# A routing stage rewritten: all x loads ahead, no mask, and GpSimd in VectorE's place for half of the normalisation

## What is computed

```python
xn = _layernorm(x)                       # (x - mean) / sqrt(var + 1e-5)
logits = xn @ gate_w.T + gate_b          # 4096 x 8
scores = softmax(logits)
top_w, top_i = top_k(scores, 2)
gate_dense = sum(one_hot(top_i, 8) * top_w[..., None], axis=1)
def expert(w1e, b1e, w3e, b3e, w2e, b2e):
    h = silu(xn @ w1e.T + b1e) * (xn @ w3e.T + b3e)
    return h @ w2e.T + b2e
y = einsum('etd,te->td', outs_of_8_experts, gate_dense)
out = x + time_mix(xn) + y + shared_expert(xn)
```

## Time and profile before

| what | us |
|---|---|
| median of 3 runs | 500.8 |
| lowest, highest | 498.76, 504.41 |
| span of the profiled execution, first to last instruction | 476.0 |
| median less that span (what lies around it) | 24.8 |
| `route` ends (`tile_tok` written) | 69.1 |

### The profile page before, as it was taken

One profiled execution on the slowest core, in us unless ns is written; L12 is line 12 of the kernel. 1 busy time (PEld: TensorE's weight loads), 2 busy tenths in 40 slices (PEclk: granted clock), 3 DMA queues, 4 the chain that ended last, 5 costly groups with the idle time before them and its releaser, 6 DMA issues.

```text
span 476.0 us, 8336 instructions
## 1 busy us (share of the span) xinstructions
PE 442.4 (93%) x2532; PEld 370.7 (78%) x2532; DVE 370.7 (78%) x700; ACT 241.5 (51%) x396; POOL 235.9 (50%) x222
## 2 busy tenths in 40 slices
PE   0886987988999999999999899999999999999997
PEld 0652464877888888888888778898898989898987
DVE  6967896968788898788776589996868687877863
ACT  4684845488586685958565633332414132423131
...
GB/s 182 281 349 330 277 88 91 105 140 180 270 232 160 216 209 185 115 152 101 145 189 122 250 323 90 228 104 152 125 148 123 121 150 132 154 108 72 23 23 44
DMA packets 45858, 77.24 MB, mean 162 GB/s; under 512 B 5908, under 2 KB 32252, under 8 KB 45820
## 3 DMA queue, kind: packets, MB, share of 16 engines
...
## 4 chain that ended last, share of the span: by engine, by line
PE 46%; POOL 17%; DVE 14%; issue 13%; ACT 4%; DMA 4%; SPq 0%; POOLq 0%; DVEq 0%; ACTq 0%
POOL xg L1008 8%; PE ps_w L1545 5%; PE ps_w L1547 5%; PE ps_w L1546 5%; PE ps_w L1611 5%; PE ps_w L1610 5%; PE ps_w L1612 5%; PE ps_g L1085 4%; DMA w_lo<-w_all 2%; POOL den L1020 2%; PE ps_y L1085 2%; POOL den L1019 2%; DVE stats L678 2%; POOL col L1027 2%; POOL firsts L1027 2%
## 5 line engine op out<-in xcount | busy, mean ns | idle before, releaser
L1008 POOL DMA_INDIRECT xg<-xn_rows,tile_tok x71 | 72.7, 1024 | 20.7 <-issue 18.5
L1521 POOL DMA_INDIRECT yg<-expert_rows,rows x64 | 67.8, 1060 | 23.6 <-issue 17.1
L1085 PE MATMUL ps_g<-w_hi,x_hi 128*128 x142 | 56.2, 396 | 1.9 <-DVE x_lo L1240 1.9
L1085 PE MATMUL ps_g<-w_lo,x_hi 128*128 x142 | 56.3, 396 | 0.0
L1085 PE MATMUL ps_g<-w_hi,x_lo 128*128 x142 | 56.1, 395 | 0.0
L1652 ACT ACTIVATE sact<-ps_w,vec_b 128x512 f32<-128x512 f32 x32 | 22.0, 687 | 58.2 <-PE ps_w L1547 58.2
L1545 PE MATMUL ps_w<-col_hi,s_hi 128*128 128x512 f32 x128 | 50.5, 395 | 0.4 <-DVE shid L1763 0.4
L1546 PE MATMUL ps_w<-col_lo,s_hi 128*128 128x512 f32 x128 | 50.2, 392 | 0.0
L1547 PE MATMUL ps_w<-col_hi,s_lo 128*128 128x512 f32 x128 | 50.2, 392 | 0.0
L1085 PE MATMUL ps_y<-w_hi,h_hi 128*128 x142 | 43.1, 304 | 1.3 <-DVE h_lo L1256 1.3
L1249 DVE TENSOR_TENSOR hid<-ps_g,act 128x512 f32<-128x512 f32 (+1 forms) x36 | 23.7, 657 | 24.6 <-ACT act L1161 24.6
...
## 6 DMA issues: line engine op xcount, KB each, us to landing
...
```

The costliest lines, as they stand in the source:

```text
L1008: pool.indirect_dma_start(out=xg[b][:, t, :], out_offset=None, in_=xn_d[:, :], in_offset=bass.IndirectOffsetOnAxis(ap=tile_tok[:, first_ti ...
L1085: mm = nc.tensor.matmul(out, x[:, k, :], w[:, ds(e, 1), k, cols].rearrange("p o n -> p (o n)"), start=(k == 0 and n == 0), stop=(last and ...
L1521: pool.indirect_dma_start(out=yg[a.buf(2)][:, k, q, :], out_offset=None, in_=y_d[:, :], in_offset=bass.IndirectOffsetOnAxis(ap=picked[a.bu ...
```

## The change

It rewrites `route` alone.

- x has 8 buffers' worth of room (`NX = NSTEP`): the four `xin`, and the two `y` buffers, `firsts1` and `terms`, lent until the experts need them. Steps 0 to 3 are loaded first, then the small inputs, then 4 to 7; only step 7 waits, for `xin[0]`.
- GpSimd scales the two groups that VectorE scaled (L508 in the changed kernel, `norm` of `gpsimd`). From step 3 on a `less_first` follows each. The zeroing of `terms` comes behind them all.
- The added 1e-5 is a bias of ScalarE's root, so VectorE's `var` operation goes. VectorE's constants come behind the statistics of step 0. Statistics have four buffers.
- There is no `mask`: TensorE sums both `hot` parts (bf16) in one accumulation, and ahead of all four `less`. The matrix `before` is 0 and -1, so that the total is subtracted in the same product. The slot is then one addition, one product of both choices and one sum.
- `share` is done once, after the one-hot rounds; ScalarE's exponents come behind its weight work, and `dense` behind `tile_tok`.
- Weight pieces are loaded up to two after each step (`SOON`).

```diff
-        NX, NN = 4, 4
+        NX, NN = NSTEP, 4
         MADE, BOTH, HIGH, LOW = 4, 6, 13, 2
         xT = [sb(f"xT{b}", [P, KC, STEP], F32) for b in range(NSTEP)]
-        xin = [sb(f"xin{b}", [P, Q, C], F32) for b in range(NX)]
+        xin = [sb(f"xin{b}", [P, Q, C], F32)[:] for b in range(4)]
+        lent = [[t[:] for t in y], [firsts1[:, b] for b in range(B)],
+                [terms[:].rearrange("p j n -> p (j n)")[:, b * HALF * C:(b + 1) * HALF * C]
+                 .rearrange("p (h c) -> p h c", h=HALF) for b in range(B)]]
+        LAST_X = NX - 1
+
+        def half(buf, b):
+            if 4 <= buf < LAST_X:
+                return lent[buf - 4][b]
+            return xin[buf % LAST_X][:, b * HALF:(b + 1) * HALF, :]
+
+        def group(buf, q):
+            return half(buf, q // HALF)[:, q % HALF, :]
+
         xn = [sb(f"xn{b}", [P, Q, C + 1], F32) for b in range(NN)]
 
-        SOON = 6
...
+        SOON = [0, 1, 2, 4, 6, 8, 10, 12, 14]
         ARRIVAL = [4, 5, 6, 7, 0, 1, 2, 3] + list(range(8, E * KC))
...
             def load_x(a):
 
-                at_least(sp, s_xn, a.i - NX + 1)
-                at_least(sp, s_xna, a.i - NX + 1)
+                if a.i == LAST_X:
+                    sp.wait_ge(s_xn, 1)
+                    sp.wait_ge(s_xna, 1)
                 for b in range(B):
-                    sp.dma_start(xin[a.buf(NX)][:, b * HALF:(b + 1) * HALF, :],
+                    sp.dma_start(half(a.buf(NX), b),
                                  xv[ds(a.i, 1), :, b, :, :].rearrange("o p h c -> p (o h) c")
                                  ).then_inc(s_xin[a.buf(NX)], 16)
 
...
-            load_x(At(0, 0, NSTEP))
-            load_x(At(0, 1, NSTEP))
+            for i in range(4):
+                load_x(At(0, i, NSTEP))
...
-            for i in range(2, NX):
+            for i in range(4, NSTEP):
                 load_x(At(0, i, NSTEP))
 
             def step(a):
...
-                if a.i + NX < NSTEP:
-                    load_x(a.plus(NX))
...
-                if a.i + SOON >= NSTEP:
-                    load_w(ARRIVAL[a.i + SOON - NSTEP])
+                for i in ARRIVAL[SOON[a.i]:SOON[a.i + 1]]:
+                    load_w(i)
...
-            nc.gpsimd.memset(terms[:], 0.0).then_inc(s_terms, 1)
-            pool.wait_ge(s_terms, 1)
-            nc.gpsimd.memset(terms[:, :, 3 * E:3 * E + 2], 1.0).then_inc(s_terms, 1)
-
             pool.wait_ge(s_negl, 32)
             nc.gpsimd.tensor_scalar(w_neg[:], w_neg[:], -1.0, None, ALU.mult).then_inc(s_neg, 1)
             pool.wait_ge(s_neg, 1)
             pool.dma_start(nw_d, w_neg[0:2 * E, :]).then_inc(s_negd, 16)
 
-            pool.wait_ge(s_negd, 16)
-            pool.wait_ge(s_lane, 4)
-            for i in range(MADE, E * KC):
+            def norm(a):
+                pool.wait_ge(s_scl, a.i + 1)
+                at_least(pool, s_T, a.i - NN + 1)
+                at_least(pool, s_xout[a.buf(NN)], a.uses(NN) * 32)
+                for q in range(DQ):
+                    ins = nc.gpsimd.tensor_scalar(xn[a.buf(NN)][:, q, 0:C], group(a.buf(NX), q),
+                                                  mv[a.buf(4)][:, q, 0:1], rstd[a.buf(4)][:, q:q + 1],
+                                                  ALU.subtract, ALU.mult)
+                ins.then_inc(s_xn, 1)
+
+            SINCE = 3
+            for i in range(NSTEP):
+                norm(At(0, i, NSTEP))
+                if i == SINCE:
+                    pool.wait_ge(s_negd, 16)
+                    pool.wait_ge(s_lane, 4)
+                if i >= SINCE:
+                    less_first(pool, MADE + i - SINCE)
+            for i in range(MADE + NSTEP - SINCE, E * KC):
                 less_first(pool, i)
+            pool.wait_ge(s_xn, LAST_X)
+            pool.wait_ge(s_xna, LAST_X)
+            nc.gpsimd.memset(terms[:], 0.0).then_inc(s_terms, 1)
+            pool.wait_ge(s_terms, 1)
+            nc.gpsimd.memset(terms[:, :, 3 * E:3 * E + 2], 1.0).then_inc(s_terms, 1)
...
-            nc.scalar.activation(early[:], gb[:], ACT.Exp)
-            exps(0, 0, EARLY)
             turned(At(0, NSTEP - 1, NSTEP))
             logit(len(GROUPS) - 1)
-            exps(1, EARLY, NSTEP)
-            act.wait_ge(s_second, 2)
-            nc.scalar.activation(gates[:, 1, :], behind[:], ACT.Exp).then_inc(s_gate, 1)
+            act.wait_ge(s_lane, 1)
+            nc.scalar.activation(lane_b[:], lane[:, :, None].broadcast_to([P, P, BATCH]), ACT.Copy
+                                 ).then_inc(s_lane, 1)
             for i in range(MADE):
                 made_hi(act, i)
             for i in range(4):
                 made_lo(act, i)
                 split(MADE + i)
-            nc.scalar.activation(early[:], gb[:], ACT.Silu)
+            nc.scalar.activation(early[:, 0:1], gb[:], ACT.Exp)
+            exps(0, 0, EARLY)
+            exps(1, EARLY, NSTEP)
+            act.wait_ge(s_second, 2)
+            nc.scalar.activation(gates[:, 1, :], behind[:], ACT.Exp).then_inc(s_gate, 1)
+            nc.scalar.activation(early[:, 1:2], gb[:], ACT.Silu)
+            act.wait_ge(s_xn, NSTEP)
+            act.wait_ge(s_xna, NSTEP)
...
+            pe.wait_ge(s_mask, 2)
+            for h, sums in enumerate((before, ones)):
+                for k in range(TOPK):
+                    mm = nc.tensor.matmul(ps_cnt[:, h, :].rearrange("p (e j) -> p e j", e=E), sums[:],
+                                          hot[:, k].rearrange("p j e -> p e j"), start=(k == 0), stop=(k == TOPK - 1))
+            mm.then_inc(s_cnt, 1)
             pe.wait_ge(s_firsts, 2)
             pe.wait_ge(s_Lg, len(GROUPS))
-            for i in range(2):
-                less(i)
-            pe.wait_ge(s_mask, 2)
-            nc.tensor.matmul(ps_cnt[:, 0, :], before[:], mask[:].rearrange("p e j -> p (e j)"),
-                             start=True, stop=True)
-            nc.tensor.matmul(ps_cnt[:, 1, :], ones[:], mask[:].rearrange("p e j -> p (e j)"),
-                             start=True, stop=True).then_inc(s_cnt, 1)
-            for i in range(2, MADE):
+            for i in range(MADE):
                 less(i)
             for i in range(4):
...
             def norm(a):
                 own = OwnIn(dve, s_dve, a, 1)
+                dve.wait_ge(s_var, a.i + 1)
                 dve.wait_ge(s_std, a.i + 1)
-                at_least(dve, s_xna, a.i - 1)
-                own.link(nc.vector.reciprocal(rstd[a.buf(2)][:], std[a.buf(2)][:]))
+                at_least(dve, s_xna, a.i - 3)
+                at_least(dve, s_xn, a.i - 3)
+                own.link(nc.vector.reciprocal(rstd[a.buf(4)][:], std[a.buf(4)][:]))
                 own.close()
-                nc.vector.scalar_tensor_tensor(out=less[a.buf(2)][:], in0=mv[a.buf(2)][:, :, 0], scalar=-1.0,
-                                               in1=rstd[a.buf(2)][:], op0=ALU.mult, op1=ALU.mult).then_inc(s_scl, 1)
-
-                at_least(dve, s_T, a.i - NN + 1)
-                at_least(dve, s_xout[a.buf(NN)], a.uses(NN) * 32)
-                for q in range(DQ):
-                    ins = nc.vector.tensor_scalar(xn[a.buf(NN)][:, q, 0:C], xin[a.buf(NX)][:, q, :],
-                                                  mv[a.buf(2)][:, q, 0:1], rstd[a.buf(2)][:, q:q + 1],
-                                                  ALU.subtract, ALU.mult)
-                ins.then_inc(s_xn, 1)
+                nc.vector.scalar_tensor_tensor(out=less[a.buf(4)][:], in0=mv[a.buf(4)][:, :, 0], scalar=-1.0,
+                                               in1=rstd[a.buf(4)][:], op0=ALU.mult, op1=ALU.mult).then_inc(s_scl, 1)
...
-                own.link(nc.vector.tensor_tensor(hot[1][:, t], work2[:, t], wide(red[:, t]), ALU.is_equal))
-                nc.vector.tensor_tensor(mask[:].rearrange("p e j -> p j e")[:, t], hot[0][:, t], hot[1][:, t],
-                                        ALU.add).then_inc(s_mask, 1)
-
-            def share(n, first_step, last_step):
-                t = slice(first_step * Q, last_step * Q)
-                count = (last_step - first_step) * Q
-                dve.wait_ge(s_exp, n + 1)
-                own.link(nc.vector.tensor_reduce(red[:, t], score[:, t], AX_X, ALU.add))
-                own.link(nc.vector.reciprocal(gates[:, 0, t], red[:, t]))
-                own.mark(nc.vector.tensor_tensor(score[:, t], score[:, t],
-                                                 gates[:, 0, t][:, :, None].broadcast_to([P, count, E]), ALU.mult))
+                nc.vector.tensor_tensor(hot[:, 1, t], work2[:, t], wide(red[:, t]), ALU.is_equal
+                                        ).then_inc(s_mask, 1)
+
+            def share():
+                dve.wait_ge(s_exp, 2)
+                own.link(nc.vector.tensor_reduce(red[:], score, AX_X, ALU.add))
+                own.link(nc.vector.reciprocal(gates[:, 0, :], red[:]))
+                own.mark(nc.vector.tensor_tensor(score, score, gates[:, 0, :, None].broadcast_to([P, NT, E]),
```

(23 more changed lines are left out.)

123 lines of the change are left out of this document (61 added, 62 removed).

## The result

| | us |
|---|---|
| the kernel before, in the runs beside it | 502.61 median (498.76 to 504.87, 4 runs) |
| the changed kernel | 511.57 median (510.26 to 512.44, 4 runs) |
| ratio, with its 95% interval | 1.0179 (1.0141 to 1.0218) |
| profiled execution of the changed kernel: time, span | 510.26, 508.4 |

A forecast was written before the change was run, and what follows sets the result against it. TensorE, busy 442.4 of 476.0 us, was taken as the bound, so only `tile_tok` mattered. No gain in the norm steps and `tile_tok` 0.8 us later gave a span of 476.8, plus 24.8, 501.6 us; range 497 to 506.

The forecast's parts named there:

- I take 0.82, since the factors come per partition as in that row: Norm steps: scaling one group on GpSimd costs 0.82 us, 1.64 a pair against VectorE's 0.73.
- GpSimd and TensorE both arriving at 35.0: End of the norm steps: both engines reach step 7 at about 35.0 us against 35.20 before, counted as no gain.
- The head: Start of the norm steps: `w_neg` issued 2.0 us later, GpSimd's first scaling at 12.6 us, TensorE beginning 2.1 us later.
- GpSimd becomes the pace: Slower rival, norm steps: GpSimd's chain has no slack; at 1.1 us a group the total is 506 us; chance 0.20.
- 1.9 us a pair: GpSimd's scaling by the Trainium skill's ratio: 2.1 us more than the sum if GpSimd paces, total 503.7 us; chance 0.07.
- Its landing took 1.35 us: Load of `w_neg`: from the last issue's end at 8.7 us, GpSimd starts to negate it at 10.0.
- twice the 0.65 us: Counts on TensorE: four matmuls instead of two take 1.25 us, from 44.8 to 46.0 us.
- TensorE in the way of the one-hot products: Between counts and one-hot products: eight weight pieces take 11.9 us, first product at 57.9 us against 56.94 before.
- TensorE warm, -1.3: Lower bound behind the counts: all four pieces at 1.48 us, first one-hot product at 56.6, 1.3 us off the total.
- The tail: From first one-hot product to `tile_tok`: VectorE's last operation ends at about 67.8, then 1.5 us, `tile_tok` at about 69.9.
- One to one into the end: Start of the experts: every microsecond `tile_tok` is ready sooner or later goes one to one into the end.
- 24.8 us above the profiled span: Whole kernel: the median of the runs is 24.8 us above the profiled span (500.8 - 476.0), kept constant.

The follow-up runs named there:

- less_late: The changed kernel with all of GpSimd's weight pieces behind its eight norm steps; ratio 1.0107 to the kernel before.
- after_fill4: The changed kernel with overwritten matrix products in TensorE's waits, one ahead of the last logits and four ahead of the counts; ratio 1.0131 to the kernel before.
- vec_fill4: The changed kernel with VectorE scaling again and overwritten products in TensorE's waits, one ahead of the last logits, four ahead of the counts; ratio 0.9958.
- no_idle1: vec_two with one overwritten matrix product in each of TensorE's two waits ahead of the counts; ratio 0.9886 to the kernel before.
- neg_early: The changed kernel with the loads of `w_neg` issued behind x steps 0 and 1, ahead of 2 and 3; ratio 1.0223 to the kernel before.
- gpsimd_only: The kernel before with only GpSimd's scaling, a weight piece after each of steps 3 to 7, and four buffers for the factors; ratio 1.0208.
- one_op: The changed kernel with one operation in GpSimd's scaling, the mean not subtracted; ratio 1.0179 to the kernel before.
- vec_scale: The changed kernel with the scaling of the two row groups given back to VectorE; ratio 1.0060 to the kernel before.
- before_again: The kernel before, unaltered, profiled a second time; span 495.0 us, time 496.7 us.
- vec_two: The changed kernel with VectorE scaling again and two of TensorE's four weight pieces ahead of the counts; ratio 0.9999 to the kernel before.

## Why the prediction was wrong, point by point

- **The step that failed: "I take 0.82, since the factors come per partition as in that row".** A group costs 1.21 us. The sum had GpSimd and TensorE both arriving at 35.0; measured, GpSimd alone sets the last turn, at 41.9. Of the 6.9 us between, the price of the scaling is 5.3: the first four pairs took 9.67 us where the sum had 7.1, and each of four cycles of pair and weight piece 4.25 where it had 3.57. The head below adds 2.2, and a weight piece that came sooner than assumed gives 0.5 back (its place of 20.5 us was itself a slip: 14.4 + 2.5 + 4 is 20.9). From there the lateness only travelled on: the counts were 6.6 us behind the forecast, the first one-hot product 7.3, `tile_tok` 7.3. The rival "GpSimd becomes the pace" named the mechanism, and its 1.1 us a group with 506 us was nearly the size; I gave it 0.20. By the forecast's own slope, 1.6 us for each 0.1, 1.21 would have made it 507.8.
- **Price and place.** Scaling at 2.42 us a pair was not the pace by itself: in less_late, with no weight pieces between, GpSimd waits for factors and TensorE sets the steps. It is pair plus weight piece in one queue, 4.25 us, and the late start. The cleanest price of who scales, in this order, is after_fill4 against vec_fill4, the same kernel but for that: 8.9 us at `tile_tok`, ratios 1.0131 and 0.9958.
- **The page.** The Trainium skill ("GPSIMD Engine Reference", section "Elementwise — side-by-side cycle accounting") gives 2.6 cycles an element on GpSimd against about one on VectorE (the 2.6 for `tensor_tensor`, with two inputs), and from it the prediction worked out 1.9 us a pair by taking cycles for time, as an estimate. The trace gives 2.42 against VectorE's 0.73, a ratio of 3.3 for this operation, so the page's side was the better one and still too low.
- **The head.** "Its landing took 1.35 us": from the end of the last issue to GpSimd's start it took 3.32 us. That and an issue 0.2 us later are the 2.2 us. It is not a fixed price: in the twelve other profiles that issue `w_neg` at this place it was 2.2 to 3.1 us, in neg_early 3.76 behind four loads only, in three profiles with the order before 1.35 to 1.7. What sets it was not tested.
- **The counts.** These were to take "twice the 0.65 us"; the four matmuls take 1.97 us. They took the same in no_idle1, at a clock of 1.00, so it isn't the clock. A bf16 product of 128x256 takes 0.49 us on `hot` rearranged; on the contiguous `mask` two took 0.6 us together (48.03 to 48.64 us before, at a low clock) and 0.4 in gpsimd_only at 1.00. That the stride does it is argued, not shown.
- **TensorE in the way of the one-hot products: right in kind, lucky in size.** 11.9 us were forecast for the eight pieces and 11.9 measured, but the other five profiles with the same queue and no fillers took 14.4 to 15.6, and after_fill4, at a full clock, 10.1. The forecast took the low clock of the kernel before, 3.4 us long, as it stood; in the change it added 1.8 to 5.5 us from execution to execution. That is likely, but not shown, to be why small gains of the norm stage (one_op, neg_early) don't show in the time.
- **"TensorE warm, -1.3".** The mechanism holds; it was too small. In vec_scale against vec_fill4 fillers cut the stretch from the counts' start to the first one-hot product from 16.4 to 12.1 us, and the ratio from 1.0060 to 0.9958 (in different groups of runs).
- **The tail.** From the first one-hot product to `tile_tok` it is 11.9 us, 12.2 before; 12.0 follows from the forecast's numbers.
- **"One to one into the end".** Only for a later `tile_tok`: 8.1 us became 9 (1.0179 of 502.6). For an earlier one, no_idle1's mix starts 3.0 us ahead of before_again's with `tile_tok` 5.6 us ahead.
- **"24.8 us above the profiled span".** Wrong in kind: a time is 1.7 to 1.9 us above its own span. It did no harm to the ratio, since I took the difference as constant.

**The account of the loss.** Given the scaling back, 1.8% becomes 0.6% (vec_scale); given two weight pieces their old place too, 0 (vec_two). The x loads, the missing mask and the rest gain about 6 us at the counts where VectorE scales, and order and clock in TensorE's queue took them back. With both mended, and TensorE's waits filled, the kernel is 1.1% under the kernel before (whose own waits were not filled in any run, so how much of the 1.1% belongs to the rewrite is not shown). Not tried together: GpSimd scaling with its weight pieces behind (less_late) and `w_neg` early (neg_early). Open: why a low clock lasts 7 us in one execution and 14 in another, and what separates the profiled execution of before from before_again in the mix.
